# A two-layer graph network on one core: a ring of score buffers, tops found in pieces, and another order of the first and the node-row loads

## The reference

```python
# layer 0: one score per edge, softmax over the edges of one src, sum of hi * att to dst
hi, hj = h[src], h[dst]
e = leaky(concat([hi, hj]) @ w, 0.2) @ a
att = exp(e) / segment_sum(exp(e), src)[src]
x = layernorm(x + segment_sum(hi * att, dst))
# layer 1: four heads of 32 channels
H = x @ W;  Hs = H . A_left;  Ht = H . A_right          # per head
s = leaky(Hs[src] + Ht[dst], 0.2);  s = exp(s - max(s))
alpha = s / (segment_sum(s, src)[src] + 1e-8)
agg = segment_sum(alpha * H[dst], src) + x @ residual_projection
x = layernorm(x + elu(agg))
```

## Time and profile before

| | |
|---|---|
| median of 3 runs | 3370.88 us (3368.73 to 3375.42) |
| profiled execution | 3371.61 us, span 3369.8 us, mean granted clock 0.968 |
| TensorE busy | 3073.6 us, 91% |
| VectorE busy | 3095.1 us, 92% |
| ScalarE busy | 2725.8 us, 81% |

### The profile page before, as it was taken

How to read it: one execution, slowest core, us unless ns; L and a number is a source line. 1 busy time by engine, 2 the same in 40 slices (tenths; PEclk the granted TensorE clock), 3 DMA queues, 4 the chain that set the end, 5 groups by cost and what they waited for, 6 DMA issues and landing times. The chain is left out here.

```text
span 3369.8 us, 100973 instructions
## 1 busy us (share of the span) xinstructions
PE 3073.6 (91%) x39974; PEld 2791.6 (83%) x39974; DVE 3095.1 (92%) x5054; ACT 2725.8 (81%) x6802; POOL 159.1 (5%) x252
## 2 busy tenths in 40 slices
PE   4777689999999999699999999987999999999995
PEld 3666577777777777599999999977999999999994
DVE  7999879998999999899999999978999999999997
ACT  4989777777877777699999999975777777777777
POOL 0000000000000000000000000000111111111110
PEclk9999899999999999799999999998999999999998
DMA  2000022222222222244333333305444445444441
GB/s 63 12 15 12 9 96 90 84 90 85 90 84 85 90 84 72 55 96 96 97 97 97 96 97 97 96 30 182 159 156 156 158 156 158 157 156 158 156 144 40
DMA packets 173164, 333.01 MB, mean 99 GB/s; under 512 B 54849, under 2 KB 108693, under 8 KB 172690
## 3 DMA queue, kind: packets, MB, share of 16 engines
q1 hardware_dynamic: 172690, 326.50, 31.6%
HBM read 320.77 MB, written 5.66 MB: 97 GB/s over the span
## 5 line engine op out<-in xcount | busy, mean ns | idle before, releaser
L942 PE MATMUL l_gathered<-xp,l_src_onehot 128*128 128x128 bf16 x7203 | 466.9, 221 | 11.2 <-DVE l_src_onehot L855 11.2
L647 PE MATMUL sc_z<-sc_onehot,pq 128*128 128x256 f32 (+1 forms) x2450 | 426.5, 296 | 54.5 <-DVE sc_leaky L568 44.9
L1316 PE MATMUL l_gathered<-hp,l_onehot 128*128 128x128 bf16 x7203 | 459.0, 219 | 0.0
L736 ACT ACTIVATE sc_leaky<-sc_z 128x1024 f32<-128x1024 f32 (+3 forms) x325 | 310.1, 954 | 153.0 <-PE sc_z L651 96.3
L942 PEld LDWEIGHTS l_gathered<-xp,l_src_onehot 128*128 128x128 bf16 x7203 | 407.8, 99 | 26.2 <-DVE l_src_onehot L855 11.6
L780 DVE TENSOR_TENSOR l_lane<-iota_b,l_lane_pairs 128x896 bf16<-128x896 bf16 x686 | 421.7, 615 | 0.0
L1330 PE MATMUL l_acc<-e,l_lane_wide 128*128 128x132 f32 x2744 | 399.3, 286 | 16.5 <-ACT e L1385 16.3
L568 DVE SCALAR_TENSOR_TENSOR sc_leaky<-sc_z,sc_leaky 128x1024 f32<-128x1024 f32 (+3 forms) x325 | 369.9, 1138 | 45.6 <-ACT sc_leaky L736 42.2
L1316 PEld LDWEIGHTS l_gathered<-hp,l_onehot 128*128 128x128 bf16 x7203 | 406.7, 98 | 0.4
L651 PE MATMUL sc_z<-sc_onehot,pq 128*128 128x256 f32 (+1 forms) x2450 | 401.0, 286 | 0.0
L647 PEld LDWEIGHTS sc_z<-sc_onehot,pq 128*128 128x128 f32 x2450 | 340.7, 194 | 69.3 <-issue 68.2
(11 more groups left out here) (233 smaller groups left out, 6064.3 us busy)
## 6 DMA issues: line engine op xcount, KB each, us to landing
l_got<-edge_rows_wide SPq DMA_DIRECT2D x343, 448.0 KB, 3.7
l_got<-edge_rows_src SPq DMA_DIRECT2D x343, 224.0 KB, 3.2
placed<-edge_rows SPq DMA_DIRECT2D x144, 512.0 KB, 3.7
out_dram<-X SPq DMA_DIRECT2D x12, 256.0 KB
edge_rows<-bin_bytes SPq DMA_DIRECT2D x98, 6.1 KB
edge_rows_wide<-bin_rows SPq DMA_DIRECT2D x98, 12.2 KB
placed<-edge_rows SPq DMA_DIRECT2D x24, 64.0 KB, 2.8
placed<-edge_rows SPq DMA_DIRECT2D x6, 256.0 KB, 3.6
```

Source lines behind the costliest of these rows:

```text
L647: nc.tensor.matmul(z[:, b, 0:nw, :], PQ[:, b0 + b, q, 0:C], hot[:, r % HOTS, b, 0, 0:nw, :], start=(b == u and q == 0), stop=False)
L736: nc.scalar.activation(y, z, ACT.Relu, scale=1.0 - ALPHA).then_inc(s["positive"], 1)
L942: ins = nc.tensor.matmul(gps[:, t % 2, i * P:(i + 1) * P], hot[:, t % RING, i, :], parts[:, g * GX + i, q, :], start=(q == 0), stop=(q == 2))
L1316: ins = nc.tensor.matmul(gps[:, t % 2, i * P:(i + 1) * P], dst_hot[:, t % RING, i, :], hp[:, g * GX + i, q, 0:C], start=(q == 0), stop=(q ...
```

## The change

- *Start.* The targets are loaded as 80 rows of 2500 instead of 125 of 1600, and every 100th is sampled. The edges of window 0, which start at edge 0, are loaded right behind them into a buffer of their own (a part of `e0`); those of window 1 as soon as the offsets are there, still in the first stage. `X` is issued by ScalarE after the targets have landed, short piece first. GpSimd no longer clears `SL`. The copies into `w1_all` stand ahead of the wait for the summed counts.
- *Binning.* `place_keys` of the first chunk is done in three pieces (two windows, two, three) instead of two.
- *Scores.* The leaky buffers are a ring of four steps; `positive` waits for the `dot` of the step four before. The short load of the thirteenth step has its own buffer and semaphore. The comparisons have three buffers instead of two. `split` is four single instructions on two engines. `slots` writes out in which step each once-a-pair task is done, earlier ones for the last pairs, and the loop ends with the last of them.
- *Layer 1.* The first three row loads are issued in `norm_and_project`. `find_top` is cut: the first four groups of scores are read two rounds earlier and lifted one round earlier, the rest at the old place. Absent pairs get their large negative number by a matrix product into the score banks (`exclude`) ahead of the scores. The sign is turned on ScalarE at the head of `exponent`.

```diff
-STEP = 64
+STEP, SAMPLED = 100, 80
...
+def load_windows(sp, k, src, dst, into, first, some, arrives):
+    with sp.Fori(some.start, some.stop) as j:
+        o = sp.value_load(k.off_i[0:1, bass.ds(j + first, 1)], min_val=0, max_val=dst.shape[0] - WIN)
+        for a, arr in enumerate((src, dst)):
+            sp.dma_start(into[:, a, bass.ds(j, 1), :],
+                         arr[bass.ds(o, WIN)].rearrange("(p a t) -> p a t", p=P, a=1)).then_inc(arrives, 16)
...
-                load(0, slice(0, FIRST), first_read)
-                load(0, slice(FIRST, CHUNK), read[0])
-                load(1, slice(0, CHUNK), read[1])
+                load_windows(sp, k, src, dst, edges[:, 0], 0, slice(FIRST, SECOND), second_read)
+                load_windows(sp, k, src, dst, edges[:, 0], 0, slice(SECOND, CHUNK), read[0])
+                load_windows(sp, k, src, dst, edges[:, 1], CHUNK, slice(0, CHUNK), read[1])
...
-                place_keys(0, slice(0, FIRST), first_read, FIRST)
+                place_keys(0, slice(0, FIRST), k.first_read, FIRST, k.first_edges)
...
-                    if n == -2:
-                        place_keys(0, slice(FIRST, CHUNK), read[0], CHUNK - FIRST)
                     if 0 <= n + 1 < NB:
                         pick(n + 1)
+                    if n == -1:
+                        place_keys(0, slice(FIRST, SECOND), second_read, SECOND - FIRST, edges[:, 0])
...
+                    if n == 0:
+                        place_keys(0, slice(SECOND, CHUNK), read[0], CHUNK - SECOND, edges[:, 0])
...
+                spread_key(1)
...
-    HOTS, EARLY = 3, 3
+    HOTS, EARLY, RING, LANES = 3, 3, 4, 3
...
-        zl = sb("leaky", [P, 2, 2, 1024])
+        zl = sb("leaky", [P, RING, 1024])
...
+        def wait_loaded(eng, r):
+            pair, j = r // PER, r % PER // 2
+            if j < 6:
+                eng.wait_ge(loaded[j % 2], 16 * (3 * pair + j // 2 + 1))
+            else:
+                eng.wait_ge(last_loaded, 16 * (pair + 1))
...
+        def slots(pair):
+            first = (pair + 1) * PER
+            if pair == PAIRS - 2:
+                at = dict(keep=3, turn=4, exponent=5, stage=5, high=6, rest=6, middle=7, low=7)
+                items = [8 + i // 2 for i in range(DEN)]
+            elif pair == PAIRS - 1:
+                at = dict(keep=2, turn=2, exponent=2, stage=1, high=2, rest=2, middle=2, low=2)
+                items = [2 + i // LANES for i in range(DEN)]
+            else:
+                at = dict(keep=3, turn=4, exponent=6, stage=7, high=7, rest=8, middle=9, low=10)
+                items = [11, 12, 12] + list(range(13, 24)) if pair < PAIRS - 3 else [11 + i // 2 for i in range(DEN)]
+            return {n: first + a for n, a in at.items()}, [first + a for a in items]
...
+                    for j in range(6):
+                        if pair >= 1 or j >= 2:
+                            used = last_group_step(pair, j - 2) if j >= 2 else last_group_step(pair - 1, j + 4)
+                            sp.wait_ge(s["hot"], used + 1)
+                            sp.wait_ge(s["away"], late_steps(used + 1))
+                        load(pair, j, 8, got[:, j % 2], loaded[j % 2])
+                    if pair >= 1:
+                        sp.wait_ge(s["hot"], last_group_step(pair - 1, 6) + 1)
+                    load(pair, 6, 1, last_got[:], last_loaded)
...
+                def take_rest(pair):
+                    n0, nw = 2 * pair, (2 if pair < PAIRS - 1 else 1)
+                    dve.wait_ge(s["part_high"], pair + 1)
...
+                    nc.vector.tensor_tensor(rest[:, 0:nw], e0[:, n0:n0 + nw, 0:NB], ep[:, pair % 2, 0:nw, :, 0], ALU.subtract
+                                            ).then_inc(s["part_rest"], 1)
...
+                def take_low(pair):
...
+                    dve.wait_ge(s["part_middle"], pair + 1)
+                    nc.vector.tensor_tensor(ep[:, pair % 2, 0:nw, :, 2], rest[:, 0:nw], ep[:, pair % 2, 0:nw, :, 1], ALU.subtract
+                                            ).then_inc(s["parts"], 1)
...
+                    if c >= LANES:
+                        dve.wait_ge(s["added"], c - LANES + 1)
...
                     act.wait_ge(s["z"], r + 1)
-                    if step % 2 == 0 and g >= 2:
-                        act.wait_ge(s["dotted"], g - 1)
+                    if r >= RING:
+                        of_pair, of_step = divmod(r - RING, PER)
+                        act.wait_ge(s["dotted"], group_of(of_pair, of_step // 2) + 1)
...
+                    act.wait_ge(s["exp"], pair + 1)
+                    if pair >= 2:
+                        act.wait_ge(s["added"], (pair - 1) * DEN)
+                    nc.scalar.copy(ep[:, pair % 2, 0:nw, :, 0], e0[:, n0:n0 + nw, 0:NB]).then_inc(s["part_high"], 1)
...
+                def take_middle(pair):
+                    nw = 2 if pair < PAIRS - 1 else 1
+                    act.wait_ge(s["part_rest"], pair + 1)
+                    nc.scalar.copy(ep[:, pair % 2, 0:nw, :, 1], rest[:, 0:nw]).then_inc(s["part_middle"], 1)
...
+def load_rows(sp, k, got, wide_rows, u):
+    b, g = divmod(u, NBK // GX)
+    sp.dma_start(got[:, u % LOADS_1].rearrange("p a x -> p (a x)"),
+                 wide_rows[g, 2 * b:2 * b + 2].rearrange("a i l -> (a i l)").partition_broadcast(P)
+                 ).then_inc(k.rows_loaded[u % LOADS_1], 16)
...
+            @block.sync
+            def _(sp):
+                for u in range(LOADS_1):
+                    load_rows(sp, k, got, wide_rows, u)
...
+                for u in range(LOADS, R):
+                    sp.wait_ge(s["hot"], u - LOADS + 1)
+                    load_rows(sp, k, got, wide_rows, u)
...
-                def find_top(b):
-                    dve.wait_ge(s["staged"], b + 1)
-                    dve.wait_ge(s["scored"], (b + 1) * PER)
+                def take_scores(b, bank, i, j):
+                    nc.vector.tensor_reduce(
+                        parts[:, i:j, :], sps[:, bank, 0:(j - i) * HP].rearrange("p (i q e) -> p i e q", q=3, e=HEADS),
+                        AX.X, ALU.add).then_inc(s["last_read" if bank else "first_read"], 1)
...
+                def lift(b, bank, i, j):
+                    dve.wait_ge(s["last_read" if bank else "first_read"], b + 1)
...
-                    nc.vector.tensor_scalar(absent[:], win[:, b % 2, :, 0], 0.0, NEVER, ALU.is_lt, ALU.mult)
-                    for bank, i, j in ((0, 0, FIRST), (1, FIRST, NB)):
-                        ins = nc.vector.tensor_reduce(
-                            parts[:, i:j, :], sps[:, bank, 0:(j - i) * HP].rearrange("p (i q e) -> p i e q", q=3, e=HEADS),
-                            AX.X, ALU.add)
-                    ins.then_inc(s["read"], 1)
...
-                    flat, sc = parts[:].rearrange("p i e -> p (i e)"), score[:, b % 2]
-                    ch.link(nc.vector.scalar_tensor_tensor(out=sc.rearrange("p i e -> p (i e)"), in0=flat, scalar=ALPHA, in1=flat,
-                                                           op0=ALU.mult, op1=ALU.max))
-                    ch.link(nc.vector.tensor_tensor(sc, sc, absent[:].unsqueeze(2).to_broadcast([P, NB, HEADS]), ALU.add))
-                    nc.vector.tensor_reduce(top[:, b % 2:b % 2 + 1], sc.rearrange("p i e -> p (i e)"), AX.X, ALU.max
+                    flat = parts[:, i:j, :].rearrange("p i e -> p (i e)")
...
+                def take_first(b):
+                    dve.wait_ge(s["scored"], b * PER + FIRST // GX)
...
+                    take_scores(b, 0, 0, FIRST)
+
+                def take_last(b):
+                    dve.wait_ge(s["scored"], (b + 1) * PER)
...
+                    take_scores(b, 1, FIRST, NB)
...
+                def find_top(b):
+                    dve.wait_ge(s["first_lifted"], b + 1)
+                    dve.wait_ge(s["last_lifted"], b + 1)
+                    if b >= 2:
+                        dve.wait_ge(s["all"], b - 1)
+                    nc.vector.tensor_reduce(top[:, b % 2:b % 2 + 1], score[:, b % 2].rearrange("p i e -> p (i e)"), AX.X, ALU.max
                                             ).then_inc(s["top"], 1)
...
-                def negate(b):
-                    dve.wait_ge(s["all"], b + 1)
-                    nc.vector.tensor_scalar(neg[:, b % 2:b % 2 + 1], k.m_all[:, b:b + 1], -1.0, None, ALU.mult
-                                            ).then_inc(s["negated"], 1)
...
+                        take_last((t + 2) // PER)
+                        lift((t + 2) // PER, 1, FIRST, NB)
                         find_top((t + 2) // PER)
...
+                    if (t + 4) % PER == 0 and 0 <= (t + 4) // PER < NB:
+                        take_first((t + 4) // PER)
...
-                    if (t + 1) % PER == 0 and 0 <= (t + 1) // PER < NB:
-                        negate((t + 1) // PER)
+                    if (t + 3) % PER == 0 and 0 <= (t + 3) // PER < NB:
+                        lift((t + 3) // PER, 0, 0, FIRST)
...
+                def exclude(b, bank, i, j):
```

(50 more changed lines are left out.)

233 lines of the change are left out of this document (108 added, 125 removed).

## The result

The changed kernel took 3280.42 us (median of 6 executions, 3277.36 to 3298.39) against 3372.45 us of the kernel before (6 executions): a ratio of 0.9741, 95% interval 0.9715 to 0.9767. The forecast was 3279 in 3252 to 3312, faster with 0.95.

A forecast was written before the change was run, and what follows sets the result against it. No engine bounds the whole: transfers hold the start, VectorE the binning, TensorE the scores and layer 1. Gains 16 + 38 + 33 + 5 = 92 us; 3371.6 − 92 − 0.7 = 3279, range 3252 to 3312.

The forecast's parts named there:

- The start: 16 forecast: Start: earlier targets, offsets and edges bring `find(2)` from 44.40 to 26.3 us; gain 16 us, 10 to 18.
- The casts, taken as gone: Start: two casts of 4.3 us fall to some 0.2 once GpSimd no longer clears `SL`; 1.4 us kept for the range.
- it lands at 14.6: Start: window 1's edges, loaded inside the first stage, land at 14.6 us, so the keys start then instead of at 26.86.
- Rival (a): Start: X's issue holds ScalarE as SyncE was (15 us), barrier stays near 21; total 3287 us, chance 0.1.
- The scores: 38 forecast: Layer 0's score stage: gain 38 us, from the pair's wait 24, the clock 10 and the end 4.
- the 1.05 forecast: Scores: TensorE's wait for `leaky` falls by 1.05 of 1.79 us a pair, over 23 pairs 24 us.
- the 10 forecast: Scores: most falls of TensorE's clock go with the shorter waits; gain 10 us, between 0 and 13.
- The ring by steps: Scores: `positive` asks for a group ended two steps before, removing its 1.54 us wait for `dot`.
- Layer 1: 33 forecast: Layer 1 loop: the 0.77 us stall at `find_top` goes, less 0.09 for new products; 49 × 0.68 = 33 us.
- rival (d): Layer 1: ScalarE's negation waits for GpSimd's all-reduce and holds TensorE; slower, 49 × 2.5 us would give 3402, chance 0.03.
- Rival (b): Layer 1 keeps half its stall because VectorE has less slack; 49 × 0.38 us lost, 3298, chance 0.12.
- The start of layer 1: 5 forecast: Start of layer 1: three of ten row loads made earlier, behind `norm_and_project`; gain 5 us, between 2 and 6.

The follow-up runs named there:

- experiment 1: The changed kernel run again with no edit, for more executions and another profile: 3281.51 us.
- experiment 2: The changed kernel with layer 1's search for tops as before (one `find_top`, absent pairs and negation on VectorE; early loads stay): 3309.80 us.
- experiment 3: The changed kernel with the whole score stage as before: 3323.32 us.
- experiment 6: The changed kernel with the last pairs' tasks and comparisons in the same steps as those of all other pairs: 3280.03 us.
- experiment 7: The changed kernel with the short load of the thirteenth step back in the two-buffer ring: 3322.02 us.
- experiment 8: The changed kernel with the leaky buffers again in two groups of two steps and ScalarE's wait group for group: 3279.95 us.
- experiment 10: The changed kernel with three unread products of 512 columns in TensorE's wait ahead of the last pair: 3278.66 us.
- experiment 4: The changed kernel with X's long piece issued at the head of the binning stage, when window 1's edges have landed: median 3285.62 us.
- experiment 9: The changed kernel with X's long piece in two: 16 blocks behind the targets, the rest after windows 2 and 3 landed: 3275.92 us.
- experiment 11: The kernel before with only the short load's own buffer and semaphore added: 3343.78 us against 3371.38.
- experiment 12: The changed kernel with X's long piece in two and three filling products ahead of the last pair, together: 3276.36 us.

## Why the prediction was right, point by point

The total was right to 1.4 us, by terms that missed in both directions: 4 us less at the start and 3.5 at the end, 8 more in the scores, and 1 either way in layer 1. Each stage gained where the forecast said it would, but that the sum met the median so closely is luck. In part so is the level: in four of eleven executions the late fall of the clock, which no term or rival named, adds 18 us.

**The start: 16 forecast, 12 measured** (10.6 to 14.4 at the first instruction of the scores in the profiles of the changed kernel and of experiments 1, 2, 3, 6, 7, 8 and 10). Targets at 7.0 for 6.0, barrier at 14.4 for 13.9: right. The casts, taken as gone, are gone: 0.23 us each; the Trainium skill's rule that a two-port cast and a GpSimd instruction exclude each other (SBUF — State Buffer, Who interferes with whom) led the forecast to 0.2, and the trace agrees. The step that failed is "it lands at 14.6": window 1's edges were there at 20.4. The 1.7 us for a load of edges came from a row in which nothing else was in flight, and here X was. Rival (a) named the danger and bound it to the wrong thing, ScalarE held by the issue; that took 0.86 us. The Trainium skill's rule that stood beside it, that loads of all queues share the same engines (DMA: Bandwidth & Descriptors, Issuing engines are not separate DMA queues), describes what happened: 7.3 us beside X, 1.7 without (experiment 4). It should have been a term of the sum. The keys started 5.8 us late and `find(2)` 4.1, for the way between them took 10.1 us instead of the 11.7 forecast; experiment 9 gives the 4.1 back.

**The scores: 38 forecast, 46.4 measured** where the clock holds. Of this the wait of TensorE is 1.09 us a pair for the 1.05 forecast, times 24 makes 26 us; right. The end gives 2.6 (13.5 to 8.6, less the 2.3 of the last pair) for 4. The term that was mis-sized is the clock: what remains is 18 us for the 10 forecast. The stage's busy times say the same, before and in experiment 8:

```profile
421.35:1364.03 942.68, 887.53 (x8657) 719.55 (x8657) 850.36 (x1102) 725.14 (x1122) 0.00 (x0) 0.97 0.26 85
```

```profile
406.93:1303.45 896.52, 868.89 (x8657) 704.05 (x8657) 835.29 (x1053) 729.22 (x1172) 0.00 (x0) 0.99 0.27 89
```

TensorE does the same 8657 products in 18.6 us less, and stands idle 27.6 us instead of 55.2. The forecast counted eight falls of the clock by the eight longest waits, and the clock of before shows these eight between 500 and 1300 us. One of them, for the others are alike:

```profile
572.00:577.00 5.00, 4.65 (x29) 3.62 (x30) 2.53 (x5) 1.97 (x4) 0.00 (x0) 0.66 0.33 102
```

A mean of 0.66 over 5 us is 1.7 us lost, 14 in eight. The forecast made 13 of them and took only 10. What it left out is a ninth fall before 500 us and the two ends of the stage, where the clock stands at 0.50 for 21 us together before and for 16 in experiment 8. In the changed kernel the clock is 1.00 until the last pair. The cause was named too broadly. The own buffer of the short load is the hinge: alone it brings 27.6 us (experiment 11), and of the 29.7 in its stage half are waits of TensorE (15.5 up to the last `leaky`) and half its clock (the same products take 14.3 us less); and without it the rest brings 5 at most (experiment 7). The ring by steps, to which the forecast gave the wait for `dot`, brings nothing (experiment 8). The 16 us between experiment 11 and the whole, most of them waits again, belong to the order of the tasks, the end, the divided `split` and the third comparison buffer together; which of them was not tried.

**Layer 1: 33 forecast, 32 measured.** By their place in the block the rounds take 2.86 to 2.91 us (medians; in the changed kernel four of 342 take 3.0 us or more, one of them 4.33 in the first block), a block 20.1 us instead of 20.8, the products that exclude absent pairs 0.06 us each, the hold of VectorE no longer reaches TensorE. ScalarE's negation waits for nothing from the second block on; rival (d) did not come. Rival (b) neither.

**The start of layer 1: 5 forecast, 6.3 measured** (4.4 to 6.7 over the profiles). The ninth one-hot starts 55.6 us after the first instruction of `norm_and_project`, 60.6 before.

**The end: 0 forecast, 3.5 lost**, where no line was changed. What VectorE waits for there is open; packets of instructions in the gap, in every late profile and in none on time, are the one thing found (below experiment 12).

## What to carry to other kernels

A long wait can cost nothing and a shorter one beside it nearly everything: in experiment 8 ScalarE waits 38.0 us for `dot` and nothing is lost, in experiment 7 it waits 20.9 us for a load and 41.8 are: there TensorE's own wait rises from 14.8 to 32.1 us and its clock falls from 1.00 to 0.97. Look at the wait of the engine that bounds the stage, not at those of the others. Where a loop has one short step, look at whose buffer it takes. A landing time read from a quiet stretch doesn't hold where a large load was moved beside it; cut the large load at what is needed first. To size what a clock costs, compare the busy time of the same products over the whole stage, its ends included; the longest waits of the middle gave 10 of 18 us.

## What the hardware showed that was not expected

- In both profiled executions of the changed kernel TensorE's clock fell to 1.2 GHz behind a wait of 0.67 us ahead of the last pair; the same wait left it at 2.4 GHz in the kernel of experiment 4, and waits of 0.70 did in the pairs before. Once down it stayed at 0.50 through 46 us of unbroken work (1272 to 1318). The trigger wasn't found.
- The stage with waits of 1.79 us a pair had a clock of 0.98, with 1.24 us (none over 1.0) it had 1.00.
- 800 KB as 125 rows had 5 packets under way at once for nine tenths of the time, and all loads together moved 99 to 176 GB/s from 3 to 10 us; as 80 rows it had up to 18 under way, and up to 290 GB/s moved.
- Two loads of 18 KB took 7.3 us beside a load of 3.2 MB issued 5 us earlier on another queue, and 1.7 us without it.
- VectorE entered the last stage 3.4 to 3.9 us late with two functions changed, and on time with either of them as before; packets of instructions moved in the gap in the ten late profiles alone.
